# A transformer block with routed experts on one core: the order of its front rewritten, the tables of slots shortened

## What is computed

```python
x = x + conv_ref(_ln_c(x), ...)        # attention over the 256 pixels of an image
t = _to_tokens(x)                      # 8 x 256 tokens of 64 channels
t = t + ffn_ref(_ln_t(t), ...)

# conv_ref
kq = einsum('kc,bcn->bkn', w_kq, xf) + b_kq        # key and query are one, 32 channels
v = einsum('vc,bcn->bvn', w_v, xf) + b_v
sim = einsum('bkn,bkm->bnm', kq, kq)
attn = softmax(sim, axis=-1)
out = einsum('ov,bvn->bon', w_o, einsum('bnm,bvm->bvn', attn, v)) + b_o

# ffn_ref: 8 experts, hidden width 682, the best two per token
probs = softmax(flat @ router_w.T)
topk_probs, topk_idx = top_k(probs, 2)             # gates: topk_probs over their sum
y = einsum('neh,ech->nec', silu(h1) * h3, w2)      # h1, h3: flat times w1, w3 of each expert
out = einsum('ne,nec->nc', gates, y)
```

## Time and profile before

| | |
|---|---|
| median of three timed runs | 175.07 us (174.26 to 176.15) |
| span of the profiled execution | 238.2 us |
| PE, DVE, ACT, POOL busy | 166.9, 99.7, 70.8, 85.7 us |
| mean granted clock of TensorE | 0.799 of 2.4 GHz |
| DMA, mean | 139 GB/s |

### The profile page before, as it was taken

How to read it: one execution, slowest core, us unless ns; L and a number is a source line. 1 busy time by engine, 2 the same in 40 slices (tenths; PEclk the granted TensorE clock), 3 DMA queues, 4 the chain that set the end, 5 groups by cost and what they waited for, 6 DMA issues and landing times.

```text
span 238.2 us, 4880 instructions
## 1 busy us (share of the span) xinstructions
PE 166.9 (70%) x1682; PEld 139.1 (58%) x1682; DVE 99.7 (42%) x372; ACT 70.8 (30%) x141; POOL 85.7 (36%) x114
## 2 busy tenths in 40 slices
PE   3595957428683069589494994958949697895683
PEld 2364836307452068588393983948839597783543
DVE  2557568255583037584222433223232344342230
ACT  2377433013310034224232142222422323333101
POOL 2963577723277700603205033060230604142400
PEclk9999586555578559979799598895997979798579
DMA  6990000184570229652958075390661600000053
GB/s 185 322 297 20 11 25 22 31 267 151 159 290 23 50 81 328 216 210 46 364 169 313 3 240 196 88 346 4 203 228 42 266 10 14 11 15 11 17 176 91
DMA packets 19893, 33.00 MB, mean 139 GB/s; under 512 B 7691, under 2 KB 13100, under 8 KB 19868
## 3 DMA queue, kind: packets, MB, share of 16 engines
q1 hardware_dynamic: 16732, 29.55, 37.8%
q0 software_dynamic: 2272, 2.35, 3.0%
q10 hardware_dynamic: 864, 0.79, 1.0%
HBM read 25.55 MB, written 7.13 MB: 137 GB/s over the span
## 4 chain that ended last, share of the span: by engine, by line
issue 48%; POOL 21%; PE 11%; DVE 8%; DMA 3%; another core or an unknown queue 3%; ACT 3%; POOLq 1%; SPq 0%; ACTq 0%; DVEq 0%
POOL ys L370 15%; POOL xs L361 5%; PE psum L925 3%; PE psum L914 2%; ACT xn L426 2%; DMA y_in<-ys 2%; DVE rows L595 1%; PE psum L894 1%; PE psum L1103 1%; PE psum L885 1%; DMA ys<-y_out,y_row 1%; DMA proj<-projections 1%; DVE index L606 1%; DVE neg_max L584 1%
## 5 line engine op out<-in xcount | busy, mean ns | idle before, releaser
L370 POOL DMA_INDIRECT ys<-y_out,y_row x39 | 37.4, 960 | 104.0 <-DVE y_out L839 95.2
L827 DVE TENSOR_TENSOR hid<-psum,act_sb 128x512 f32<-128x512 f32 (+1 forms) x50 | 33.4, 676 | 88.9 <-ACT act_sb L504 61.6
L1031 PE MATMUL psum<-x_cols,weights 64*128 64x128 f32 x390 | 52.9, 286 | 13.9 <-issue 12.1
L1031 PEld LDWEIGHTS psum<-x_cols,weights 64*128 64x128 f32 x390 | 47.6, 193 | 19.4 <-issue 15.8
L1033 PE MATMUL psum<-x_cols,weights 64*128 64x128 f32 x390 | 53.1, 286 | 0.9 <-issue 0.9
L504 ACT ACTIVATE act_sb<-psum 128x512 f32<-128x512 f32 (+1 forms) x50 | 28.7, 586 | 70.0 <-remote 42.4
L1033 PEld LDWEIGHTS psum<-x_cols,weights 64*128 64x128 f32 x390 | 47.7, 193 | 1.1 <-issue 1.1
L1059 PE MATMUL psum<-hid,weights 128*64 128x128 f32 x468 | 42.8, 357 | 2.1 <-issue 1.1
L1059 PEld LDWEIGHTS psum<-hid,weights 128*64 128x64 f32 x468 | 39.3, 189 | 4.8 <-issue 2.7
L361 POOL DMA_INDIRECT xs<-xrows,pos x32 | 31.6, 987 | 12.9 <-issue 8.9
L1037 PE MATMUL psum<-x_cols,weights 64*106 64x128 f32 x78 | 8.7, 349 | 23.1 <-ACT act_sb L504 18.4
(11 more groups left out here) (148 smaller groups left out, 189.9 us busy)
## 6 DMA issues: line engine op xcount, KB each, us to landing
weights<-experts SPq DMA_DIRECT2D x39, 565.0 KB
xs<-zeros SPq DMA_DIRECT2D x4, 1040.0 KB, 11.1
x_in<-xs SPq DMA_DIRECT2D x39, 32.5 KB
ys<-y_out,y_row POOLq DMA_INDIRECT x39
xs<-xrows,pos POOLq DMA_INDIRECT x32
y_in<-ys ACTq DMA_DIRECT2D x2, 256.0 KB, 4.5
y_in<-ys SPq DMA_DIRECT2D x2, 256.0 KB, 4.3
x_sb<-x_tok SPq DMA_DIRECT2D x1, 384.0 KB, 3.4
```

The costliest lines, as they stand in the source:

```text
L370: nc.gpsimd.indirect_dma_start(ys, bass.IndirectOffsetOnAxis(ap=y_row[:, j:j + 1], axis=0), y_out[:, i % RING, h, :], None).then_inc(y_sca ...
L827: nc.vector.tensor_tensor(live(i, hid[:, i % 2, s, :]), live(i, H3_BANK[g % 3]), live(i, act_sb[:, g % 3, :]), ALU.mult).then_inc(hid_done, 1)
L1031: first_ = nc.tensor.matmul(H1_BANK[g % 2][:, src], weights[0:C, slot, P * s:P * (s + 1)], x_cols[0:C, i % 2, src], start=True, stop=True)
```

## The change

It does six things.

- PE's list in pairs 1 to 3: `similarity` of the next pair ahead of the attention of the odd image; the turned probabilities and the values of a pair ahead of the rank of the pair before; six of the idle matmuls are gone. The rank now waits for the copy of the values, and the odd attention for the rank's reading.
- DVE's list: the row maxima of the next pair's images between and behind the two residuals; `t_statistics` behind `positions` (pairs 1 to 3); `normalise_t(2)` behind pair 3's statistics; `normalise_t(1)` behind the tables of phase 0.
- ACT: the exponentials of image 2 ahead of the normalisation of pair 3.
- POOL: `t_deviation(1)` one scatter later.
- SP: each of the first four weights is issued as soon as its owner is read.
- The tables take fewer instructions: the first row of a slot is found by adding up jumps between owners, and phase 1's last steps move into the steps of quad 0, phase 2's jumps into quad 1.

```diff
                 sp.wait_ge(dispatched[p], 16 * TPP * K_TOP * (KNOWN[p] - (KNOWN[p - 1] if p else 0)))
 
             sp.wait_ge(table_ready, 1)
-            load_weights(0, owners_of(0))
+            for h in members(0):
+                owner = sp.value_load(table[0:1, 0, h:h + 1], min_val=0, max_val=E - 1)
+                sp.dma_start(weights[:, h, :], experts[bass.ds(owner, 1)].rearrange("o p c -> p (o c)")).then_inc(w_loaded[h], 16)
             early_rows, second_owners = [rows_of(0), rows_of(1)], owners_of(1)
             landed(0)
             load_rows(0, early_rows[0])
...
             for p in range(PAIRS):
                 for at in range(TPP * K_TOP):
-                    if p == 0 and at == TPP * K_TOP - 2 or p == 2 and at == K_TOP:
+                    if p == 0 and at == TPP * K_TOP - 1 or p == 2 and at == K_TOP:
                         t_deviation(p + 1)
                     scatter_row(p, at)
                 if p == 1:
...
+            exponentials(2)
             normalise(3)
             for p in range(1, PAIRS):
-                exponentials(2 * p)
+                if p >= 2:
+                    exponentials(2 * p)
...
             def owners_of_slots(p):
                 own = slice(OPENED[p], OPENED[p + 1])
                 n = OPENED[p + 1] - OPENED[p]
-                chain(nc.vector.tensor_scalar(given[:], ends[:], float(SUB), None, ALU.mult))
-                end = given[:, 0:E - 1].unsqueeze(1).to_broadcast([P, n, E - 1])
                 chain(nc.vector.tensor_tensor(passed[:, own, :], slot_at[:, own].unsqueeze(2).to_broadcast([P, n, E - 1]),
-                                              end, ALU.is_ge))
-                chain(nc.vector.tensor_reduce(owner[:, own], passed[:, own, :], AX.X, ALU.add))
-                nc.vector.tensor_copy(table[:, 0, own], owner[:, own]).then_inc(dve_step, 1)
+                                              ends[:, 1:E].unsqueeze(1).to_broadcast([P, n, E - 1]), ALU.is_ge))
+                with nc.allow_low_precision(reason="numbers of experts: whole and below 2^3"):
+                    nc.vector.tensor_reduce(table[:, 0, own], passed[:, own, :], AX.X, ALU.add).then_inc(dve_step, 1)
                 steps[0] += 1
-                chain(nc.vector.tensor_tensor(starts[:, own, :], passed[:, own, :], end, ALU.mult))
-                chain(nc.vector.tensor_reduce(first[:, own], starts[:, own, :], AX.X, ALU.max))
-                chain(nc.vector.tensor_tensor(row_at[:, own], slot_at[:, own], first[:, own], ALU.subtract))
+
+            def jumps_between_owners(p):
+                if p == 0:
+                    chain(nc.vector.tensor_scalar(jump[:], full[:, 0:E - 1], -float(SUB), float(CAP), ALU.mult, ALU.add))
+                    return
+                chain(nc.vector.tensor_tensor(begin[:], used[:, p - 1, :], base[:], ALU.add))
+                chain(nc.vector.tensor_tensor(begin[:], begin[:], ends[:, 0:E], ALU.subtract))
+                chain(nc.vector.tensor_tensor(jump[:], begin[:, 1:], begin[:, 0:E - 1], ALU.subtract))
 
             def rows_of_slots(p):
                 own = slice(OPENED[p], OPENED[p + 1])
                 n = OPENED[p + 1] - OPENED[p]
-                all_e = [P, n, E]
+                chain(nc.vector.tensor_tensor(starts[:, own, :], passed[:, own, :],
+                                              jump[:].unsqueeze(1).to_broadcast([P, n, E - 1]), ALU.mult))
+                chain(nc.vector.tensor_reduce(row_at[:, own], starts[:, own, :], AX.X, ALU.add))
                 if p == 0:
-                    nc.vector.scalar_tensor_tensor(out=table[:, 1, own], in0=owner[:, own], scalar=float(CAP),
-                                                   in1=row_at[:, own], op0=ALU.mult, op1=ALU.add).then_inc(table_ready, 1)
+                    nc.vector.tensor_tensor(table[:, 1, own], row_at[:, own], slot_at[:, own], ALU.add
+                                            ).then_inc(table_ready, 1)
                     return
-                chain(nc.vector.scalar_tensor_tensor(out=begin[:], in0=used[:, p - 1, :], scalar=float(SUB), in1=base[:],
-                                                     op0=ALU.mult, op1=ALU.add))
-                chain(nc.vector.tensor_tensor(of_owner[:, own, :], order[:].unsqueeze(1).to_broadcast(all_e),
-                                              owner[:, own].unsqueeze(2).to_broadcast(all_e), ALU.is_equal))
-                chain(nc.vector.tensor_tensor(starts_e[:, own, :], of_owner[:, own, :],
-                                              begin[:].unsqueeze(1).to_broadcast(all_e), ALU.mult))
-                chain(nc.vector.tensor_reduce(owned[:, own], starts_e[:, own, :], AX.X, ALU.add))
-                chain(nc.vector.tensor_tensor(owned[:, own], owned[:, own], row_at[:, own], ALU.add))
-                nc.vector.tensor_scalar(table[:, 1, own], owned[:, own], float(E * CAP - SUB), None, ALU.min
+                chain(nc.vector.scalar_tensor_tensor(out=row_at[:, own], in0=row_at[:, own], scalar=begin[:, 0:1],
+                                                     in1=slot_at[:, own], op0=ALU.add, op1=ALU.add))
+                nc.vector.tensor_scalar(table[:, 1, own], row_at[:, own], float(E * CAP - SUB), None, ALU.min
                                         ).then_inc(table_ready, 1)
...
             for p in range(PAIRS):
-                if p == KNOWN[0]:
-                    subtiles_of_experts(0)
-                    owners_of_slots(0)
-                    rows_of_slots(0)
                 if p >= 1:
                     x_logits(p)
                 residual(2 * p)
                 tops(2 * p)
+                if 1 <= p < PAIRS - 1:
+                    row_max(2 * p + 2)
                 residual(2 * p + 1)
-                t_statistics(p)
-                if p + 1 < PAIRS:
-                    row_max(2 * p + 2)
+                if p == 0:
+                    t_statistics(0)
+                    row_max(2)
                 tops(2 * p + 1)
                 choose(p)
                 carry_on(p)
+                if 1 <= p < PAIRS - 1:
+                    row_max(2 * p + 3)
+                positions(p)
+                if p >= 1:
+                    t_statistics(p)
+                if p == 0:
+                    normalise_t(0)
+                    row_max(3)
+                if p == KNOWN[0] - 1:
+                    subtiles_of_experts(0)
+                    owners_of_slots(0)
+                    jumps_between_owners(0)
+                    rows_of_slots(0)
+                    normalise_t(1)
                 if p == PAIRS - 1:
-                    pair_up(0)
-                positions(p)
-                if p == PAIRS - 1:
-                    used_up(0)
-                    subtiles_of_experts(1)
-                    owners_of_slots(1)
-                    rows_of_slots(1)
-                    pair_up(1)
-                normalise_t(p)
-                if p + 1 < PAIRS:
-                    row_max(2 * p + 3)
+                    normalise_t(2)
+            pair_up(0)
+            used_up(0)
+            subtiles_of_experts(1)
+            owners_of_slots(1)
+            pair_up(1)
+            normalise_t(3)
...
             def tables_between(i, s):
-                if (i, s) == (0, 5):
+                if (i, s) == (0, 1):
+                    jumps_between_owners(1)
+                elif (i, s) == (0, 2):
+                    rows_of_slots(1)
+                elif (i, s) == (0, 5):
                     used_up(1)
                     subtiles_of_experts(2)
                 elif (i, s) == (1, 1):
                     owners_of_slots(2)
+                elif (i, s) == (1, 2):
+                    jumps_between_owners(2)
                 elif (i, s) == (1, 3):
                     rows_of_slots(2)
...
+            def ranks_read(n):
+                pe.wait_ge(rank_read, n)
+                pe.wait_ge(counts_ready, sum(k <= n for k in KNOWN))
+
             def value_out(p):
                 if p >= 1:
                     pe.wait_ge(u_ready, p)
                     pe.wait_ge(t_ready, 2 * p)
-                    pe.wait_ge(rank_read, p)
-                    pe.wait_ge(counts_ready, sum(k <= p for k in KNOWN))
+                    ranks_read(1 if p == 1 else p - 1)
...
             for p in range(1, PAIRS):
-                if p >= 2:
-                    keep_busy(3)
-                rank(p - 1)
+                if p == 1:
+                    rank(0)
                 transpose_probs(2 * p)
                 value_out(p)
+                if p >= 2:
+                    rank(p - 1)
                 if p + 2 < PAIRS:
                     transpose_x(p + 2)
                 attend(2 * p)
                 transpose_probs(2 * p + 1)
                 if p + 2 < PAIRS:
                     key_query(p + 2)
-                attend(2 * p + 1)
                 if p + 1 < PAIRS:
                     similarity(p + 1)
+                attend(2 * p + 1)
             keep_busy(4)
             rank(PAIRS - 1)
```

58 lines of the change are left out of this document (29 added, 29 removed).

## The result

The change makes the kernel slower. The first measurement gave 179.97 us (179.28 to 181.08, 4 runs) against 174.66 (173.95 to 176.15, 4 runs): ratio 1.0288, 95% interval 1.0209 to 1.0366. Over all executions of the study the medians are 179.28 us (15 runs) and 175.94 (57 runs): 1.9%, 3.3 us. The forecast was +2.8 us.

What follows compares the result with a forecast made beforehand. PE bounds the experts' part, so quad 2's start counts, which waits for the second group's rows. Front -3.2, scatters +6.3, shorter tables some 0.3 back: +2.8 on 175.07 gives 177.9 us, range 171.3 to 180.3.

Steps and rivals of the forecast that it cites:

- (5): Pair 2's scatters on POOL: all eight stand behind the deferred normalise_t(2), costing 6.3 us on the path quad 2 waits for.
- (1, 2): Front: reordered PE and ACT lists gain nothing yet; moved row maxima and normalise_t(2) bring the last image's rows 3.2 us earlier.
- both ends, 2.0 and 4.6: Cases for the front's gain: with 4.6 us the kernel is +1.5 us, with 2.0 it is +4.3.
- (3): Tables on DVE: first hid 10.0 us behind the last image's rows, with a new wait of about 1 us for POOL.
- (4): SP's first weights issued one by one, and POOL's hole of 3.6 us in pair 1 from t_deviation(1) later: each worth 0.
- (6): Six fillers fewer on PE: they took no one's time, though the clock in pairs 2 and 3 may fall; 0.
- (2): Front on DVE: row maxima between residuals and normalise_t(2) behind pair 3 bring the last image's rows 3.2 us earlier.
- Who comes last at quad 2: Start of quad 2: before, PE at 82.9 and weights at 83.0 are level; changed, PE ready at 84.9, weights at 86.1.
- The check that gave 175: Kernel before: quad 2 at 83.0, 7 x 9.5, about 7.2 for the last quad and 18.3 to the end make 175.
- Rival A: Quad 2: PE, not the second group, decides in both versions; faster, 172.7 or 171.3 us; chance 0.24.
- The row that could lengthen it: Pair 2's scatters held behind quad 1's weights on the DMA engines: up to 3.4 us added if still streaming.

Runs made afterwards that it cites:

- e8: The changed kernel measured again on another chip: 178.77 us, ratio 1.013 to the kernel before.
- e1: The changed kernel with normalise_t(2) back early, between image 6's top values and image 7's residual: 174.12 us, ratio 0.984 to the kernel before.
- e2: The kernel before with one edit, normalise_t(2) deferred behind pair 3's positions: 182.23 us, ratio 1.037.
- before: The kernel without the change; its profile rows come from a second profile without pauses. Pooled median 175.94 us.
- b0: The kernel before, unchanged, run once more for a profile without the two pauses: 175.19 us, ratio 1.000.
- after: The changed kernel in its first measurement and profile: 179.97 us, ratio 1.029 to the kernel before.
- e10: The kernel before with only the change's shorter tables, order unchanged: 176.94 us, ratio 1.000.
- e4: The changed kernel with t_statistics(1) back ahead of image 3's top values: 177.65 us, ratio 1.017 to the kernel before.
- e11: The changed kernel with normalise_t(2) early again and the six fillers of pairs 2 and 3 put back: 175.57 us, ratio 0.999 to the kernel before.
- e5: e1 plus t_deviation(3) behind pair 2's eight scatters, normalise_t(3) in quad 0, second table's row numbers ahead of pair_up(1): 174.41 us, ratio 0.978 to the kernel before.
- e7: The kernel before with t_deviation(3) behind pair 2's eight scatters and normalise_t(3) in quad 0's third step: 176.15 us, ratio 1.002.
- e9: e5 plus e4's edit, t_deviation(1) one scatter earlier and normalise_t(1) ahead of the first table: 174.15 us, no ratio given.

## Why the prediction was right

The sign, the place and the size held. Against the pooled medians the forecast of +2.8 us is 0.5 short; against the first measurement, +5.3, it is half, and by e8 it is right. Point by point:

**The second group sets the end, by the scatters (5).** This carried the forecast and is shown, by e1 and e2 from both sides. Rows out come at 72.71 against 72.2 forecast, in before at 69.45 against 69.1. Behind them the kernel is a fixed length: in every kernel with the late second group, from rows out to the last down are 85.5 to 87.2 us (six profiles). The shift of 3.26 us in rows out stands beside 3.3 in the pooled time; that it fits so well is luck, since rows out of e8 against b0 give only 1.05 (these two executions differ by 1.2 us, 177.78 and 176.57, and those of after and b0 by 4.5). Against R, which both profiles agree on, the deferral moved the last scatter by 5.1 us (R + 10.3 to R + 15.4) where 6.3 were forecast: the first started at R + 3.8 for R + 4.2, and t_deviation(3) took 1.6 us between two scatters (61.93 to 63.49), not 2.2. Both terms of the sum, this one and the front's gain in the first profile, were over a microsecond too large, and their errors cancel.

**The front ends earlier (1, 2).** Right in kind: DVE waits for POOL's rstd_t 1.26 us in b0 and no more after. Forecast gain 3.2 us; the profiles give 1.9 (after) and 4.0 (e8). The same kernel differs by 2 us with the clock that it is granted, so the size can't be read closer. The prediction had both ends, 2.0 and 4.6, and took the middle. By the terms of its own sum these ends give +4.0 and +1.4, not +4.3 and +1.5.

**Shorter tables (3).** First hid 64.46 for 64.5, by luck: it came at R + 8.9 and not R + 10.0, and R was 1.1 us later than forecast. The DVE wait for t_deviation(3) was 0.33 us, not 1. Worth 0 alone (e10): right.

**Weights one by one, the hole in pair 1 (4): 0.** Right for the hole, and for the reason given: SP is with its reads when pair 1 lands, and stands 0.6 us for it in b0 and in after. The hole comes from two moves and not from the one I named (e4). The weights one by one were in no run by themselves; their 0 is argued.

**Fillers (6): 0.** Wrong. "They took no one's time" is so in before, where the probabilities came late. In the new order they would hold PE up by 1.28 us in pair 2 (e11), so their removal is a gain that the forecast doesn't have, by some 0.7 us at the rows of image 4. Where it ends up, in the front's gain of (2) or nowhere, no run shows.

**Who comes last at quad 2.** In before: near. PE came last in b0 by 1.4 us, at the long table in quad 1, where I had put 82.9. So rows that come up to 1.4 us later cost nothing in before. The deferral passes that point by 1.9 us and more: the shorter tables in quad 1 took PE's lateness away. After: the forecast had quad 2 start when its weights land, with PE ready 1.2 us before. PE waited for no weights there, in neither profile, since the low clock behind its stand, which the prediction doesn't have, made it that much later. The check that gave 175 for the kernel before came out by luck: a quad costs 8.97 us and not 9.5, against a later quad 2 and a longer end.

**Rival A** (PE decides in both) falls by e2 and e1 together. **The row that could lengthen it**, scatters held behind the weights' stream: 0 in after, since the stream is over by 66.5 and the last scatter at 70.97, landed 1.7 later. It is real where scatters are earlier: in e5 SP goes on 4.2 us behind the last one in place of 1.7. The Trainium skill ("DMA: Bandwidth & Descriptors", SWDGE vs HWDGE vs iDMA) has an engine take the two kinds of queue in turn, and I had read that as no delay. e5's trace agrees with the turns, 174 packets of the software queue among 859 of the hardware queue from 57 to 65.6, but not with my reading: 5.6 us from issue to landing there and 2.4 outside the stream (e1, 63 to 66).

What stays open: why rows out to the last down is 89.2 us in e7 (behind rows out PE waits 1.1 us for weights, 1.6 for rows and 1.3 for the long table), and how much of e1's 1.6%, which stands on four runs and an interval of 0.971 to 0.996, comes from the fillers.

## What to carry to other kernels

When work is deferred behind a later stage, ask which in-order queue it feeds, and count that queue's whole backlog from the new start: here 1.1 us of DVE work moved past two residuals, and eight scatters moved with it. Look for a gap in the same engine's list before deferring: 2.11 us of DVE idle ahead of the last residual took `normalise_t(2)` at no cost, and turned a loss of 1 to 3% into a gain of 1 to 2%. Where several arrivals are within a microsecond or two of each other (scatters, table, weights, PE), shortening one moves the wait to the next: e5, e7 and e10 each gained on their own term and little or nothing at the end. And look for what the waiting engine does in its own list before it waits: in e9 SP was reading values, and no earlier scatter could help.

## What was not expected of the hardware

Identical instructions in the front took 2 us more or less between executions, with the granted clock at 0.50 or 0.94 from 30 to 40 us. PE's clock was still high at the start of a 3.7 us stand and dropped behind it (0.59 over 6.3 us, 0.73 in e8), and fourteen fillers inside the stand kept it at 1.00, which the kernel could not use. A scatter's end in the profile is not its landing: 1.7 us before SP goes on when the engines are free, 4.2 when 565 KB loads stream.
